# Attention items of the full TensorE array put behind the two value blocks of an even slot

## What is computed

```python
kv_c = rms(x @ W_kv) * g_kv;  q_c = x @ W_q
k_rope = rope(x @ W_krope);   q_rope = rope(q_c @ W_qrope)
scores = einsum('bhqd,bhkd->bhqk', q, k) * scale      # causal, softmax
out = einsum('bhqk,bhkd->bhqd', attn, v) @ W_o
x = x + ga * out
h = layernorm(x) * (1 + cb) + sb;  t = (h @ Wm + bm) as heads of 32
top two of softmax(t @ expert_emb) choose experts of gelu(t @ W1 + b1) @ W2 + b2
x = x + gb * (comb @ Wo + bo)
```

## Time and profile before

| | |
|---|---|
| median of 3 runs | 2947.76 us (2946.74 to 2962.08) |
| span of the profiled execution | 2947.5 us |
| PE busy | 2823.2 us (96%) |
| DVE busy | 1869.7 us (63%) |
| ACT busy | 1806.7 us (61%) |
| POOL busy | 1243.5 us (42%) |
| granted PE clock, mean | 0.991 |

### The profile page before, as it was taken

How to read it: one execution, slowest core, us unless ns; L and a number is a source line. 1 busy time by engine, 2 the same in 40 slices (tenths; PEclk the granted TensorE clock), 3 DMA queues, 4 the chain that set the end, 5 groups by cost and what they waited for, 6 DMA issues and landing times.

```text
span 2947.5 us, 51530 instructions
## 1 busy us (share of the span) xinstructions
PE 2823.2 (96%) x16460; PEld 1254.0 (43%) x16460; DVE 1869.7 (63%) x4636; ACT 1806.7 (61%) x2148; POOL 1243.5 (42%) x1325
## 2 busy tenths in 40 slices
PE   6789999999999999999999999999999999999999
PEld 2344444444444444444434444444444444444433
DVE  5665766756667566666666666675756657666553
ACT  1346675566755667456674576655766566655687
POOL 4311555126551364413644146531465225661254
PEclk9889999999999999999999999999999999999999
DMA  6303443034430444204432044321553124531243
GB/s 141 73 1 84 113 121 96 4 98 112 133 73 2 106 123 118 70 8 119 121 100 70 21 128 122 90 56 29 134 130 91 34 63 115 130 84 27 74 129 93
DMA packets 177556, 253.06 MB, mean 86 GB/s; under 512 B 51085, under 2 KB 83869, under 8 KB 177197
## 3 DMA queue, kind: packets, MB, share of 16 engines
q1 hardware_dynamic: 170300, 247.79, 32.9%
q10 hardware_dynamic: 6996, 1.99, 0.3%
HBM read 159.13 MB, written 12.63 MB: 58 GB/s over the span
## 4 chain that ended last, share of the span: by engine, by line
PE 85%; DVE 6%; issue 3%; ACT 2%; POOL 1%; SPq 0%; DMA 0%; ACTq 0%; DVEq 0%; POOLq 0%
PE ps L1236 17%; PE ps L1272 17%; PE ps L1290 16%; PE ps L1256 9%; PE ps L418 8%; PE ps L464 4%; PE ps L505 2%; PE ps L466 2%; PE ps L535 2%; DVE front L561 1%; PE ps L516 1%; DVE rest L1392 1%; PE ps L492 1%; PE ps L523 1%; PE ps L450 1%
## 5 line engine op out<-in xcount | busy, mean ns | idle before, releaser
L1356 ACT ACTIVATE rest<-ps 128x1024 f32<-128x1024 f32 x1024 | 993.7, 1024 | 341.2 <-PE ps L1272 341.1
L1338 ACT ACTIVATE rest<-ps 128x1024 f32<-128x1024 f32 (+3 forms) x768 | 608.6, 810 | 550.1 <-PE ps L1236 536.4
L1456 POOL TENSOR_TENSOR rest<-rest 128x512 f32<-128x512 f32 x478 | 631.9, 1322 | 560.6 <-DVE rest L1392 550.1
L1392 DVE SCALAR_TENSOR_TENSOR rest<-ps,b2c,wide 128x512 f32<-128x512 f32 x512 | 383.8, 750 | 490.4 <-PE ps L1290 460.7
L1272 PE MATMUL ps<-wide,w1s 98*128 98x512 f32 x2048 | 644.6, 434 | 11.5 <-ACT rest L1356 8.7
L1290 PE MATMUL ps<-rest,w2s 128*32 128x512 f32 x4096 | 546.1, 605 | 0.6 <-ACT rest L1356 0.6
L1446 POOL TENSOR_SCALAR_AFFINE_SELECT rest<-rest 128x256 f32<-128x256 f32 x512 | 204.3, 407 | 806.7 <-ACT rest L1338 803.6
L558 DVE CUSTOM_DVE_ANT_0 rest<-ps,maskd 128x256 f32<-128x256 f32 (+3 forms) x1024 | 458.7, 487 | 121.9 <-PE ps L418 114.6
L1236 PE MATMUL ps<-wide 49*128 49x512 f32 (+3 forms) x2304 | 485.7, 511 | 7.2 <-ACT rest L1338 6.1
L1272 PEld LDWEIGHTS ps<-wide,w1s 98*128 98x128 f32 x2048 | 346.0, 189 | 238.4 <-ACT rest L1356 109.4
L561 DVE TENSOR_REDUCE front<-ps 128x1 f32<-128x512 f32 x512 | 329.1, 685 | 103.7 <-PE ps L418 99.9
(11 more groups left out here) (138 smaller groups left out, 2225.0 us busy)
## 6 DMA issues: line engine op xcount, KB each, us to landing
wide<-gate_rows SPq DMA_DIRECT2D x1024, 128.0 KB, 2.8
wide<-front SPq DMA_DIRECT2D x480, 64.0 KB, 2.0
wide<-front SPq DMA_DIRECT2D x192, 128.0 KB, 2.4
ao<-in_x SPq DMA_DIRECT2D x16, 512.0 KB, 5.0
heads<-front SPq DMA_DIRECT2D x64, 128.0 KB, 2.4
xs<-in_x SPq DMA_DIRECT2D x16, 512.0 KB, 5.1
out<-xs SPq DMA_DIRECT2D x32, 256.0 KB, 2.7
wide<-ao SPq DMA_DIRECT2D x96, 64.0 KB, 2.3
```

The source lines that it names most:

```text
L1338: nc.scalar.activation(L.pt[:, u % PTS, :, f:HALF], L.ps[:, 2 * (u % 2):2 * (u % 2) + 2, 0:HALF - f], ACT.Exp, scale=SCALE).then_inc(S["c_ ...
L1356: nc.scalar.activation(L.hm[:, u % HM, :], bank(2 * (u % 2), 2), ACT.Gelu).then_inc(S["e_gelu"], 1)
L1392: v.scalar_tensor_tensor(out=dst, in0=bank(L2 + q % 2), scalar=L.b2c[:, e:e + 1], in1=L.gb[:, q // 2 % GB, q % 2, :], op0=ALU.add, op1=ALU ...
L1456: g.tensor_tensor(dst, dst, L.gy[:, k % GY, :], ALU.add).then_inc(S["e_add"], 1)
```

## The change

A slot gets a fourth list, `after`, which PE issues behind the two value blocks (or at the slot's end). The full-array items move there, mostly to even slots; DVE, ACT and POOL process them last in the slot.

- ropes 9 to 15 go from slots 2, 3, 4, 5, 6, 7, 8 to the ends of slots 2, 4, 4, 6, 6, 8, 8; rope 8 stays in slot 0
- `out` 2, 3: slot 1 to slot 2; `sums` of a stretch: from two slots after its last to three after
- `tr`: 27, 28 to 28, 28; `o`: 32, 33 to 30, 32; `tr2`: 37, 37 to 36, 36; `tm`: 38, 39 to 38, 38; `lg` and `gt` stay in slots 40 and 46, behind the values
- the `row` items and all pairs keep their places (in slots 4 and 8 a pair that stood behind a rope is now ahead of it)

```diff
-    slots = [([], [], []) for _ in range(NM)]
+    slots = [([], [], [], []) for _ in range(NM)]
     if img:
-        slots[1][1].extend([("out", 2), ("out", 3)])
+        slots[2][3].extend([("out", 2), ("out", 3)])
...
-    ropes = {s: ("rope", 8 + k) for k, s in enumerate((0, 2, 3, 4, 5, 6, 7, 8))}
...
-        if part and img and s and s in ropes:
-            slots[s][1].append(ropes.pop(s))
         slots[s][part].append(pair)
-    for s, rope in ropes.items():
-        slots[s][1].append(rope)
+    slots[0][1].append(("rope", 8))
+    for k, s in enumerate((2, 4, 4, 6, 6, 8, 8)):
+        slots[s][3].append(("rope", 9 + k))
...
-        slots[last + 2][2].append(("sums", m))
-    slots[27][1].append(("tr", 0, 0))
-    slots[28][1].append(("tr", 0, 1))
-    slots[32][1].append(("o", 0, 0))
-    slots[33][1].extend([("o", 0, 1), ("stats", 0)])
+        slots[last + 3][3].append(("sums", m))
+    slots[28][3].extend([("tr", 0, 0), ("tr", 0, 1)])
+    slots[30][3].append(("o", 0, 0))
+    slots[32][3].extend([("o", 0, 1), ("stats", 0)])
     slots[34][1].append(("xn", 0))
-    slots[37][1].extend([("tr2", 0, 0), ("tr2", 0, 1)])
-    slots[38][1].append(("tm", 0, 0))
-    slots[39][1].extend([("tm", 0, 1), ("tlo", 0, 0)])
-    slots[40][1].extend([("tlo", 0, 1), ("lg", 0), ("chain", 0, 1), ("chain", 0, 2)])
+    slots[36][3].extend([("tr2", 0, 0), ("tr2", 0, 1)])
+    slots[38][3].extend([("tm", 0, 0), ("tm", 0, 1), ("tlo", 0, 0)])
+    slots[40][1].append(("tlo", 0, 1))
+    slots[40][3].extend([("lg", 0), ("chain", 0, 1), ("chain", 0, 2)])
...
-    slots[46][2].append(("gt", 0))
+    slots[46][3].append(("gt", 0))
...
                     if s and s % 2 == 0:
                         values(img, s - 2)
                         values(img, s - 1)
+                    for item in after:
+                        item_matmuls(pe, L, RA[img], item)
...
-                    for item in between + behind + front:
+                    for item in between + behind + front + after:
```

More of the change, by code:

```diff
@@ L1295, in _ @@
             for img in range(B):
-                for s, (between, behind, front) in enumerate(aslots[img]):
+                for s, (between, behind, front, after) in enumerate(aslots[img]):
                     scores(img, s, 0)
```

## The result

The changed kernel takes 3042.29 us (median, 3030.83 to 3048.09), the one before 2949.2 us beside it: a ratio of 1.0303, interval 1.028 to 1.0325. The forecast was 2998, range 2955 to 3020. The direction is right; the loss is 93 us where 50 were forecast.

A forecast was written before the change was run, and what follows sets the result against it. PE was taken to bound the kernel, 85% of the last-ending chain, at full clock after the opening. Images 1 to 7 lose +6.5 us each, 45.5, plus 4.4 for image 0: 50 on 2947.5, median 2998 us, range 2955 to 3020.

The forecast's parts named there:

- The switch: Each change of PE's array shape costs about 0.2 us; 14 fewer switches save 2.8 us an image.
- Slots 1 to 8: Waits behind moved ropes and `out` lose 5.6 us against 10 x 0.2 won: +3.6 us an image.
- The 0.5 for exponentials: Slots 5 and 6: with nothing between them, PE waits some 0.5 us for exponentials.
- the 1.8 of slots 1 to 4: Waits for exponential and mask 0.7, slot 4's pair for its bank 0.8, `values(3)` for its mask 0.3: 1.8 us.
- Rival (a): New waits stay hidden, under 2.8 us an image, and switches decide: 21 us saved, 2926 us; chance 0.09.
- Slots 17 to 20: `sums` no longer waits behind `row` for DVE, but the next pairs meet the same DVE work: 0.
- 21 to 24: Slot 22's gate products run later on DVE behind `sums`; slot 24's first pair waits 1.6 us: +1.5 in all.
- Slots 29 to 35: `o` ahead of slots 31 and 33 makes pairs of 32 and 33 wait 0.75 and 1.05; other waits go: +0.8.
- 38/39: Both `tm` ahead of slot 39 make slot 40 wait 1.2 us for its exponential, less two switches: +0.8.
- 41/42: Bare slots wait for ACT once the cover that `sums` gave goes; one switch saved: +0.2 us.
- the late terms (2.9): Image 0: the later slots' terms cost 2.9 us, added to early about +1.5; 4.4 together.
- Rival (c): Waits chain further because a late mask delays the exponentials three slots on: 3025 us or more; chance 0.07.

The follow-up runs named there:

- experiment 2: Changed kernel with GpSimd (POOL) doing the items of `after` behind the next slot's mask, PE's order kept: 3016.94 us, ratio 1.0207.
- Experiment 3: Changed kernel with DVE doing the five gate products of slot 22 ahead of the items of `after` (`sums`): 3018.98 us, ratio 1.0207.
- experiment 4: Changed kernel with POOL's items behind the next mask, DVE's gate products ahead of `after`, and the second `tm` back in slot 39: 2981.84 us, ratio 1.0093.
- experiment 7: Kernel before with the first `tr2` of slot 37 between its two scores, two more switches an image: 2959.16 us, timed once.
- Experiments 1: Changed kernel with ropes 9 to 15 back in their old slots, one to a slot ahead of the values: 3010.16 us, ratio 1.0184.
- experiment 6: The kernel of experiment 4 with `sums` 2 and 3 back beside their `row` in slots 17 and 21: 2975.1 us, ratio 1.0067.
- experiment 5: Kernel before with only `sums` 2, 3, 4 moved to the ends of slots 20, 24, 26 and both `tr` to the end of 28: 2959.2 us, ratio 1.0019.
- experiment 8: Kernel before with only `sums` 4 moved to the end of slot 26 and both `tr` to the end of 28: 2952.07 us, ratio 0.9997.

## Why the prediction was right in sign and short in size

**What bounds the kernel** held: a microsecond that PE lost was a microsecond of the end, and experiments 2 to 4 gave it back. "The granted clock is full after the opening" was a misreading: the kernel before goes at 1.2 GHz for 24.9 us in the attention of image 0.

**The switch** held: 0.2 forecast, 0.18 measured by experiment 7 in the slot itself. In place it is worth 0.13 (slots 25 to 28) or nothing (slots 9/10, one switch fewer and +0.14). The rope of four passes that the price is taken from is rope 11, not 12, which changes nothing.

**Slots 1 to 8** held: +3.6 against +3.95, with the waits of `values(3)`, `values(5)`, `values(7)` and slot 7's pair at 0.33, 0.85, 0.68 and 1.00 against 0.3, 1.0, 0.8 and 1.2. The 0.5 for exponentials was too high (0.18), and the 1.8 of slots 1 to 4 can't be taken apart in the trace. Experiments 1 and 2 show the ropes and POOL's order as the cause. Rival (a), waits hidden, is refuted: the waits that the trace shows in slots 4 to 8 alone (0.33, 0.18, 0.85, 1.00, 0.68) come to 3.0 us, over its 2.8. The strict FIFO queues that the prediction takes from the Trainium skill (TensorE: Matmul & The Clock Gate, its opening table) fit what experiment 2 shows: the mask moved ahead of the ropes in POOL's program, and the waits ended.

**Slots 17 to 20 and 21 to 24.** "The next pairs meet the same DVE work, 0" came to +0.22, and +1.5 to +1.7: held while the clock is full.

**Slots 29 to 35** were too high (+0.8 against +0.23): the pairs of slots 32 and 33 wait 0.13 and 0.72, where 0.75 and 1.05 were forecast. **38/39** was +0.8 against +1.15 and **41/42** +0.2 against +0.39. These errors nearly cancel.

**The step that failed is "Sum for images 1 to 7: 3.6 + 1.5 - 0.6 + 0.8 + 0.2 + 0.8 + 0.2 = +6.5 us each, 45.5".** The seven terms came to 7.6, 53.5 us. An eighth was missing: 2.5 us an image, 17.3 in all, that PE loses at 1.2 GHz. Its granted clock of 0.991 was read as given, and not as something that the new order could change. Experiment 3 took the wait in slot 24 away and the stretches around 24 and 25 went; experiment 6 put the sums back and those in 18 and 22 went too; experiment 5 brought slot 18's back on the old kernel (images 3 and 6) with `sums` and `tr` moved, and experiment 8, the same without `sums` 2 and 3, had none. So the wait of slot 24 brings the stretches behind it, and moving `sums` out of slots 17 and 21 those in 18 and 22. What it is in that move is open, for PE idles about as long there before; and so is why image 3 has the half clock in slot 18 and image 2, with the same waits, has not.

**"image 0 has the late terms (2.9) and early about +1.5"**, 4.4, came to 16.8. The granted clock in three stretches of its attention, behind which it is full up to the experts (at 294.26 after, 273.69 before); after:

```profile
92.40:150.00 57.60, 50.62 (x275) 22.02 (x279) 34.78 (x110) 23.36 (x29) 27.01 (x34) 0.93 0.36 79
150.00:200.00 50.00, 43.59 (x228) 19.41 (x221) 28.01 (x86) 15.20 (x22) 8.13 (x20) 0.66 0.00 1
200.00:253.70 53.70, 48.16 (x286) 22.06 (x284) 35.66 (x101) 23.51 (x29) 5.19 (x11) 0.90 0.01 1
```

and before:

```profile
88.63:144.00 55.37, 51.25 (x287) 21.80 (x289) 34.66 (x110) 23.47 (x30) 26.99 (x34) 0.96 0.36 83
144.00:194.00 50.00, 42.50 (x269) 19.99 (x265) 35.69 (x107) 19.72 (x29) 8.94 (x22) 0.83 0.01 1
194.00:233.00 39.00, 36.70 (x223) 16.41 (x221) 26.60 (x79) 18.37 (x22) 4.27 (x9) 0.96 0.00 1
```

A length times what its clock lacks of 1.00 is the most that a stretch can have lost by it: 4.0 + 17.0 + 5.4 = 26.4 us after, 2.2 + 8.5 + 1.6 = 12.3 before. The difference, 14 us, would cover the 12.4 that the forecast lacks; but it is an upper bound, and new waits (1.1 for the mask of slot 7, 1.3 for the heads of slot 8, 2.7 for DVE in slot 23) overlap with it. In experiment 4 image 0 is down to +4.8. Experiment 7 gives a measure of the clock alone: its image 0 is that of the kernel before but for one `tr2`, goes at 1.2 GHz for 36.0 us there in place of 24.9, and takes 4.4 us longer. So some of the 12.4 can differ from one execution to the next; how much of it is clock and how much waiting was not separated.

**The rest:** 3.8 us of the difference lie in the opening, where no instruction was moved. In the ten traces of this study slot 0 of image 0 starts between 88.6 and 93.5 us; the profile before has the earliest, and the least time at 1.2 GHz ahead of it. The expert parts, which no edit touched, differ from those before by -0.1 to +6.0 us. Together 50 + 8.0 (terms) + 17.3 (clock) + 12.4 (image 0) + 3.8 (opening) + 2.2 (expert parts) = 93.7, to rounding the 93.5 us.

**Rival (c)** named 3025 or more at 0.07, by masks that delay exponentials three slots on. The time is there, but that is not how: in images 1 to 7 the waits did not chain beyond the forecast, and the clock made most of the difference. The range assumed waits of at most 130% of the forecast (3022); it had no term for anything that the waits cause.

## What to carry to other kernels

Before moving an item past a neighbour, write out each other engine's queue behind it: a second rope in the batch put 2.6 us of POOL's work ahead of the mask that PE asks for next, and reordering only the helper's queue ended that wait. A filler between two steps of the bound engine can cover a neighbour's latency; removing it moves the wait, it does not end it. And where a trace shows the bound engine's clock falling behind new waits, as here, count a new wait twice: its own length, and the work behind it at the lower clock, from the granted clock of the slots around it.

## What was not expected of the hardware

- Two idle times of 0.5 and 0.4 us of PE within some 2 us (slot 18) were followed in some images by 3.41 us at 1.2 GHz, and by none in others with the same instructions; 16 passes of 512 columns then took 3.00 us against 1.71. Moving `sums` out of slot 17 was enough to bring this (experiment 5); with `sums` in its place, idle times of 0.47 and 0.45 us some 2.4 us apart brought none.
- The opening, up to the first attention slot, is the same in all ten kernels and varied by 5 us between their executions, and the expert parts by 6 us: as much as most of the single terms summed here. Differences of a few microseconds are to be read from slots, not from the span.
